# Products of the identity in nine of TensorE's waits between the dense expert layer and the routed one

## What is computed

```
x = x + L0_conv(layernorm_over_channels(x))        # window attention
t = tokens(x)
t = t + L0_ffn(layernorm(t))                       # 8 experts, computed densely, top 2 kept
x = image(t)
h = groupnorm(conv1(layernorm(x)))                 # L1_conv: 128 -> 32 channels, 16 groups
z = relu(groupnorm(conv3d(h) + depthwise9x9(h)))   # the taps
z = relu(groupnorm(conv2(z)))                      # 32 -> 128 channels
x = x + (z + layernorm(x))
t = tokens(x)
t = t + L1_ffn(layernorm(t))                       # 16 experts, top 2 of a softmax over logits
```

## Time and profile before

| | us |
|---|---|
| median of three runs | 718.04 |
| lowest and highest of them | 716.93, 719.39 |
| the profiled execution | 720.16 |
| its span in the profile | 718.3 |
| PE busy | 563.4 |
| POOL busy | 423.9 |
| DVE busy | 357.8 |
| ACT busy | 355.7 |

### The profile page before, as it was taken

The page is one execution under the profiler, slowest core; times in us unless marked ns, Lnnn a source line. Parts: engine busy times, 40 slices in busy tenths (PEclk is TensorE's granted clock), DMA queues, the critical chain, the costliest instruction groups (busy, mean ns, idle before and its releaser), DMA issues.

```text
span 718.3 us, 16000 instructions
## 1 busy us (share of the span) xinstructions
PE 563.4 (78%) x5352; PEld 467.6 (65%) x5353; DVE 357.8 (50%) x1040; ACT 355.7 (50%) x843; POOL 423.9 (59%) x484
## 2 busy tenths in 40 slices
PE   2677788868599999999996689836269999999900
PEld 2565677657377776677774468515169999999900
DVE  6977778646600611210024454582756555555523
ACT  4476687975573536641144522224036665666600
POOL 1677798765774786753343000077567777777771
PEclk9999999899997999999995597855569999999965
DMA  9452222111364452322580000011223332333536
GB/s 298 147 143 78 82 75 83 51 52 49 128 218 162 156 187 106 111 110 85 185 249 0 1 0 1 0 48 50 67 60 107 100 96 86 108 97 96 198 113 212
DMA packets 59039, 75.30 MB, mean 105 GB/s; under 512 B 9470, under 2 KB 49366, under 8 KB 58302
## 3 DMA queue, kind: packets, MB, share of 16 engines
q1 hardware_dynamic: 51614, 60.49, 27.1%
q0 software_dynamic: 5632, 11.62, 4.8%
q10 hardware_dynamic: 1728, 2.36, 0.9%
HBM read 57.96 MB, written 23.81 MB: 114 GB/s over the span
## 4 chain that ended last, share of the span: by engine, by line
PE 60%; DVE 13%; POOL 8%; ACT 8%; issue 7%; DMA 3%; SPq 1%; POOLq 0%; DVEq 0%; ACTq 0%
PE bank L800 13%; PE bank L762 9%; PE bank L861 8%; PE bank L745 8%; PE bank L811 7%; PE bank L722 3%; PE bank L316 3%; ACT normed L906 3%; POOL gathered_or_att L570 2%; POOL padded_or_w L561 2%; POOL returned L640 2%; PE bank L791 2%; PE bank L760 1%; POOL gathered_or_att L579 1%; DVE ln_stats L1092 1%
## 5 line engine op out<-in xcount | busy, mean ns | idle before, releaser
L605 POOL TENSOR_TENSOR padded_or_w<-padded_or_w,gathered_or_att 128x384 f32<-128x384 f32 x96 | 95.5, 1001 | 74.9 <-ACT padded_or_w L980 71.2
L621 POOL DMA_INDIRECT sorted_x<-normed,slot x72 | 71.3, 990 | 101.6 <-DVE slot L1323 80.4
L640 POOL DMA_INDIRECT returned<-gathered_or_att,home_of_slot x104 | 102.7, 988 | 31.7 <-issue 22.6
L980 ACT ACTIVATE padded_or_w<-bank,moe_b 128x384 f32<-128x384 f32 x96 | 55.4, 579 | 101.0 <-PE bank L745 100.7
L762 PEld LDWEIGHTS bank<-moe_or_conv,padded_or_w 128*128 128x128 f32 x576 | 82.0, 200 | 31.3 <-issue 10.4
L762 PE MATMUL bank<-moe_or_conv,padded_or_w 128*128 128x128 f32 x576 | 85.2, 287 | 0.0
L745 PE MATMUL bank<-chan_major,moe_or_conv 128*128 128x384 f32 x192 | 82.5, 516 | 0.0
L1352 DVE TENSOR_TENSOR att_or_moe<-att_or_moe,bank 128x256 f32<-128x256 f32 x104 | 43.7, 420 | 50.2 <-PE bank L811 26.8
L994 ACT ACTIVATE att_or_moe<-bank 128x256 f32<-128x256 f32 x104 | 39.9, 383 | 57.0 <-PE bank L800 56.5
L660 PE MATMUL bank<-padded_or_w 64*64 64x64 f32 x1152 | 48.1, 235 | 25.3 <-issue 17.0
L660 PEld LDWEIGHTS bank<-padded_or_w 64*64 64x64 f32 x1152 | 42.0, 147 | 34.9 <-issue 34.9
(11 more groups left out here) (179 smaller groups left out, 1092.3 us busy)
## 6 DMA issues: line engine op xcount, KB each, us to landing
gathered_or_att<-combine SPq DMA_DIRECT2D x24, 768.0 KB, 4.2
padded_or_w<-windows SPq DMA_DIRECT2D x192, 48.0 KB, 1.9
sorted_x<-in_pad_rows SPq DMA_DIRECT2D x26, 260.0 KB, 7.2
padded_or_w<-sorted_x SPq DMA_DIRECT2D x26, 260.0 KB
padded_or_w<-in_moe_w SPq DMA_DIRECT2D x8, 512.0 KB, 5.3
qy<-returned SPq DMA_DIRECT2D x6, 384.0 KB, 4.8
out<-residual ACTq DMA_DIRECT2D x12, 192.0 KB, 2.1
normed<-returned SPq DMA_DIRECT2D x6, 384.0 KB, 5.4
```

Of the source, the lines that this page charges most:

```text
L605: nc.gpsimd.tensor_tensor(HB[n % DRING], HB[n % DRING], GB_[k % 3][:, n % 4, :], ALU.mult).then_inc(S("gated"), 1)
L621: nc.gpsimd.indirect_dma_start(xs_dram[b], bass.IndirectOffsetOnAxis(ap=POS[b][:, k, t:t + 1], axis=0), TNR[b][:, t, :], None).then_inc(S( ...
L640: nc.gpsimd.indirect_dma_start(yt_dram[b], bass.IndirectOffsetOnAxis(ap=HOMES[b][:, j:j + 1], axis=0), YR[k * RING + j % RING], None).then ...
L980: nc.scalar.activation(HB[n % DRING], banks[HBANK[n % 2]][:, 0:DG], ACT.Gelu, bias=B1C[:, e:e + 1]).then_inc(S("gelu"), 1)
```

## The change

A new function on PE, `keep_clock`, first waits for a semaphore and then issues a number of products of the identity (128 by 128, fp32) with itself into the first 128 columns of bank 3, which nobody reads. Nine phases `KW` of it are put into the list: 24 products behind the dense layer and the first four up products of image 0, 10 and 12 around image 1's first statistics product, 6 ahead of its second, 30 ahead of its third and 10 behind that, 18 ahead of image 1's routing transposes, 34 behind its logits, and 16 behind its prefix products. The semaphore says that bank 3's last reader is done (`gelu`, `hc_ready` or `up_out` at its last count). The products signal no semaphore, and nothing else changes.

```diff
--- before.py
+++ after.py
@@ -235,12 +235,12 @@
             *every(56, 2, groups("AN", "XL", 0)), (61, ("XC", 0)), (62, ("XCE", 0)), (62, ("GN", "XC", 0)), (65, ("GS", "XC", 0)), (67, ("GQ", "XC", 0)),
             (69, ("XCH", 0)), *every(71, 1, taps(0, 0, 54)), (89, ("GN", "XM", 0)), (91, ("GS", "XM", 0)), (93, ("GQ", "XM", 0)), (95, ("XMH", 0)),
             *every(96, 1, [("XU", 0, n) for n in range(4)])])
-        order += [*normed("XL", 1), *[("XU", 0, n) for n in range(4, 8)], ("GN", "XU", 0), *groups("XG", 1), ("GS", "XU", 0), ("GQ", "XU", 0),
-                  ("XC", 1), ("XCE", 1), ("GN", "XC", 1), ("GS", "XC", 1), ("GQ", "XC", 1), ("XCH", 1), *groups("XUH", 0),
+        order += [("KW", 24, "gelu", DN), *normed("XL", 1), *[("XU", 0, n) for n in range(4, 8)], ("GN", "XU", 0), *groups("XG", 1), ("GS", "XU", 0), ("GQ", "XU", 0),
+                  ("XC", 1), ("XCE", 1), ("GN", "XC", 1), ("KW", 10, "hc_ready", 2 * NB), ("GS", "XC", 1), ("GQ", "XC", 1), ("XCH", 1), ("KW", 12, "hc_ready", 2 * NB), *groups("XUH", 0),
                   *taps(1, 0, 9), *groups("XZ", 0), *groups("AN", "XL", 1), *taps(1, 9, 24), *routing(1, 0), *taps(1, 24, 54),
-                  *choice(1, 0, 1, 6), ("GN", "XM", 1), ("GS", "XM", 1), ("RP", 0), ("GQ", "XM", 1), ("XMH", 1), ("RS", 0),
-                  *[("XU", 1, n) for n in range(8)], ("GN", "XU", 1), ("GS", "XU", 1), ("GQ", "XU", 1), *groups("XUH", 1), *groups("XZ", 1),
-                  *routing(1, 1), *choice(1, 1, 1, 6), ("RP", 1), ("RS", 1),
+                  *choice(1, 0, 1, 6), ("GN", "XM", 1), ("KW", 6, "hc_ready", 2 * NB), ("GS", "XM", 1), ("RP", 0), ("GQ", "XM", 1), ("XMH", 1), ("RS", 0),
+                  *[("XU", 1, n) for n in range(8)], ("GN", "XU", 1), ("KW", 30, "up_out", 8 * NB), ("GS", "XU", 1), ("GQ", "XU", 1), ("KW", 10, "up_out", 8 * NB), *groups("XUH", 1), *groups("XZ", 1),
+                  ("KW", 18, "up_out", 8 * NB), *routing(1, 1), ("KW", 34, "up_out", 8 * NB), *choice(1, 1, 1, 6), ("RP", 1), ("KW", 16, "up_out", 8 * NB), ("RS", 1),
                   *[("M", b) for b in range(NB)], *[("F", b) for b in range(NB)]]
 
         group_no = {ph: k for k, ph in enumerate(ph for ph in order if ph[0] in ("LNA", "YA", "RT", "LG", "RX", "XG", "XZ"))}
@@ -825,6 +825,11 @@
 
                 tile_groups(pe, b, step, 4)
 
+            def keep_clock(n, bank_free, count):
+                pe.wait_ge(S(bank_free), count)
+                for k in range(n):
+                    nc.tensor.matmul(banks[3][:, 0:P], IDN, IDN, start=True, stop=True)
+
             def group_stats(name, b):
 
                 n, mat = gns.index((name, b)), G8 if name == "XU" else G2
@@ -881,7 +886,7 @@
                 pe_group(pe, group_no[("XZ", b, g)], [QY[b][:, (g * TG + k) * P:(g * TG + k + 1) * P] for k in range(TG)])
 
             run(LNA=lambda *w: normed_group(pe, "LNA", *w), A=lambda n: attend(att, n), YA=attended, RT=lambda *w: normed_group(pe, "RT", *w), LG=logits, RX=comb_rows,
-                D=dense, RP=route_b, M=moe, XG=lambda *w: normed_group(pe, "XG", *w), XC=conv1, XT=taps, GS=group_stats, XU=conv2, XZ=conv_sum)
+                D=dense, RP=route_b, M=moe, XG=lambda *w: normed_group(pe, "XG", *w), XC=conv1, XT=taps, KW=keep_clock, GS=group_stats, XU=conv2, XZ=conv_sum)
 
 
         @block.scalar
```

## The result

Over 20 executions of each kernel on the same chips the changed one took a median of 716.38 us (707.23 to 723.57) and the one before 718.88 (713.75 to 721.45): the ratio is 0.9934, with a 95% interval of 0.9907 to 0.9960. That ratio leaves out executions more than 1.5% above the fastest of their kernel, seven of the changed kernel's and none of the other's; the means over all twenty, 716.11 and 718.48, differ by 2.4 us, or 0.33%. The change makes the kernel a little faster: 0.66% by the ratio, 0.33% by the means. Its times spread wider than before; why is not shown.

A forecast was written before the change was run, and what follows sets the result against it. PE's dependence chain was taken to bound the kernel: PE waits, then works at half clock. Terms 0.6 + 2.0 - 0.3 - 0.9 - 0.8 - 0.35 = +0.25 us on the median 718.04 gave 718.3; range 713.0 to just short of 722.0.

The forecast's parts named there:

- The price of a product: Each filler product, fp32 128x128 by 128x128, takes 0.222 us at full clock and 0.46 at half.
- The overruns: Fillers ending behind their waits: the thirty +2.0 us (+1.4 to +2.5), the 34 +0.85; the 6, second 10 and 16: 0.
- I take half clock: The ten behind conv1 start at half clock, so the statistics product ends 2.9 us late; at full clock +0.5.
- my three signs of being wrong: Wrong if: clock full at the thirty's start; logits mostly at full clock; PE idle ahead of statistics products after the fillers.
- no filler lies there: 0: Transposes of image 0's sum, taps 9 to 54 and image 0's routing: change 0, with 1.1 us either way.
- the gains that I put behind the filler of 18: Image 1's routing transposes -0.9 us and its logits -0.8 us (0 to -3.9 if all at full clock).
- The term for the front: Fillers of 24, 10 and 12 together: +0.6 us; -1.7 if the ten run at full clock, +1.6 with conv1 at half.
- its own w: Time of one tap record at full clock, 0.25 us (2w at half), from eighteen records at image 1's first taps.
- The clock holds: Rival, chance 0.27: short waits after fillers no longer drop the clock; -6.4 us, 711.6, or 713.0 with the thirty cold.
- The clock rises late: Rival, chance 0.23: rise 5.7 us after every cold start, fillers of 10, 30 and 34 end late; +4, 722.0.
- the fillers don't raise it: Rival, chance 0.04: fillers leave the clock at half; the thirty alone +6.7 us, sum above +10, 728 or more.
- The rule on transposes: Transposes don't engage full clock as other products do; conv1 then meets half clock, sum +1.25; weighed and not adopted.

The follow-up runs named there:

- the kernel with the six alone: The changed kernel with only the six fillers behind the taps (6, 30, 10, 18, 34, 16), without 24, 10 and 12; ratio 1.0023 to the kernel before.
- the two kernels with ten cold products: The changed kernel with only the fillers of 24, 10 and 12 (ratio 0.9962), and the changed kernel without its filler of 24 (ratio 0.9976).
- the second and third trace of before: The kernel before, unaltered, traced twice more; 719.86 and 720.90 us in one execution each.
- the four traces of unaltered code: Three traces of the kernel before, stretches 149.9, 146.3 and 146.3 us, and one with only a filler of 16 at the routed layer's start, 149.8.
- the second set: The changed kernel unaltered, run again against the kernel before; means over all twelve times 716.5 and 717.0 us, ratio 0.9953.
- the three front fillers alone: The changed kernel with only the fillers of 24, 10 and 12, the other six removed; ratio 0.9962 to the kernel before.
- all but the 24: The changed kernel without its filler of 24 alone; ratio 0.9976 to the kernel before.
- the mended kernel: Kernel before with fillers through all waits, but no 24 and none between conv1's transposes, 32 behind the prefix products, 8 at the routed layer's start; ratio 0.9867, median 709.62 us.

## Why the prediction was wrong

The forecast was 718.3, no change, within 713.0 to 721.8. The median lies inside, but the kernel moved, by more than its interval, the way to which I gave 0.30.

*The price of a product* held: 2.50 us for ten at full clock, 4.43 to 4.57 at half. *The overruns* held: the thirty put the statistics product 1.6 us late (18.05 us behind the second one, 16.49 before; I had +2.0, at least +1.4), 0.6 us late in the kernel with the six alone; the 34 and the prefix products together gave -0.6 (-0.35 forecast; +0.6 and -1.2 measured one by one); the statistics product and what follows up to the first transposes gave the -0.3 forecast, and the transposes of image 1's sum up to its routing another -0.4, for which I had no term; the 6, the second 10, the 18 and the 16 cost nothing.

*The first step that failed* is "I take half clock" for the ten behind conv1. At full clock I had -1.7 for the front, at half clock +0.6, or +1.6 with conv1 slow too. The front as a whole, from the first up product to the sum's transposes, takes 35.2 us after the change, for 37.2 and twice 37.0: -1.8 to -2.0. The runs show all three cases: conv1 to the sum's transposes is 14.7 before (14.3 in the later traces), 12.3 in the changed kernel, and 15.0 to 15.2 in the two kernels with ten cold products, one of them with a conv1 late by 2 us besides. Image 1's first taps run at full clock in all five traces with the ten and the twelve, and from the statistics product to the sum's transposes it is 7.8 us for 10.5 to 10.9; against that the statistics product comes 0.7 us later behind conv1 where the ten meet full clock, and 3.4 to 3.6 where they meet half. So the mechanism was right; the state of the clock at that point was not to be read from one fall at 402.7: in the second and third trace of before it falls 2.8 us later in the same work. What decides between the two states stays open. None of my three signs of being wrong named this place: the clock was half at the start of the thirty, image 1's logits ran at half clock, and no idle time was left ahead of the statistics products behind the ten and the thirty.

*The second* is "no filler lies there: 0" for the stretch from the sum's transposes to image 0's logits. It took 18.1 us in every trace without the front fillers, and 17.5 or 16.5 in every trace with the change's. In the kernel before the clock is up too when the transposes that VectorE paces begin (it rose at 412.9), but it falls as taps 9 to 24 begin (at 419.8 in the first trace), and they take 9.18. In the changed kernel it falls 1.9 us ahead of them, among the last of those transposes, and is back 1.5 us into them: 8.27. In the kernels with 16.5 it doesn't fall there at all, and they take 7.51. So a gain came in a stretch where nothing was changed; that the full-clock taps ahead bring it fits all these traces, but no run here tests it alone.

*The third* are the gains that I put behind the filler of 18: -0.9 for the routing transposes and -0.8 for image 1's logits. Both were 0: 3.08 and 7.86 us as before. The filler of 18 met full clock (the clock was up from 470.6 on), but the clock fell at 491.1, while PE waited 2.18 us for ScalarE, ahead of both. The kernel that fills that wait too has its logits at 4.19.

Adding up against the mean of the four traces of unaltered code (148.1 for the stretch): up to image 0's logits 52.7 for 55.2, -2.5; from there to the second statistics product 24.0 for a mean of 24.0, 0; behind it +0.3. That is -2.2, and the means of the first set of times say -2.4. The agreement is in part luck. Two of the four hold the long form of image 0's logits; with the kernel of the six behind the taps, unaltered up to there, as a fifth, the mean of 24.0 becomes 23.6 and the sum -1.8. And the means of the second set say -0.4, the ratio of the first -4.7. The runs show where the gain lies, and its size only within these bounds. The term for the front was the one that decided. One size in it was off as well: by its own w, 18 tap records at full clock are 4.5 to 4.6 us, not 4.4, and they took 4.5 to the next product. The trace of before that I read happened to hold the slow form of the logits, which the forecast did not need, but which made the two profiles look 4.0 us apart.

*The rivals.* "The clock holds" had the right sign, but not its means: the clock did not hold behind the taps, and the thirty did not fit. "The clock rises late" and "the fillers don't raise it" fell: in the changed kernel it rose 2.7 to 4.8 us into the fillers that started cold; only with the three front fillers alone did the 24 wait 5.7 us for it, and that kernel was late up to image 0's logits (56.0 us, before 55.4).

*The rule on transposes* (the Trainium skill, TensorE: Matmul & The Clock Gate, "Part 4: PE-mode transpose") is not borne out by the changed kernel either: the clock rose at 402.3, when PE had done nothing but transposes since 398.7. The rise does not always come: with the same eighteen at half clock, the clock rose within them or 0.1 us behind them in eight of ten traces, and not in the traces of all but the 24 and of the mended kernel.

## What to carry to other kernels

A filler on a throttled engine pays by the clock that the next long work on the chain meets, so it has to end just before that work: price it at the clock it will start at, and leave nothing idle behind it. Where waits follow each other, fill all of those between a filler and the work it is for, since one wait of 2 us left empty took the clock back here, and leave out fillers ahead of work whose length does not decide. A single trace shows one way in which the clock can fall; before reading a gain of some us from two traces, take the kernel before a second time and count from mark to mark.

## What the runs showed of the hardware

The same code differs by 3.3 us between executions with the place at which the clock falls: 0.8 us into the logits or at their end. It does not look freely drawn: two traces of the changed kernel, of executions of equal time, agree within 0.1 us in each part, and logits with the taps behind them took 24.0 us in all five traces with the change's two fillers around the statistics product, and 22.3 or 25.6 in the five without any filler ahead of the taps. What sets the place is not shown. Logits of 16 columns ran for 7.86 us at half clock without lifting it, although PE was busy throughout, and image 0's saw it fall while they ran; eighteen fp32 transposes lifted it in eight traces of ten.
